# Attention with heads of 16: set-up fills, root, norm, queries and idle products put in other places

## The reference

```python
y_dca, y_main = y[:, -DCA:, :], y[:, :-DCA, :]        # DCA = 16
kv_dca = (y_dca @ Wkv_dca + bkv_dca).reshape(b, DCA, 2, H, HD)
k_dca, v_dca = _ln(kv_dca[:, :, 0], kn_dca_w, kn_dca_b), kv_dca[:, :, 1]
q = _ln((x @ Wq + bq).reshape(b, s1, H, HD), qn_w, qn_b)
kv = concat([y_main @ Wk + bk, y_main @ Wv + bv]).reshape(b, s2, H, 2 * HD)
k, v = _ln(kv[..., :HD], kn_w, kn_b), kv[..., HD:]
out = (attn(q, k, v) + attn(q, k_dca, v_dca)) @ Wo + bo   # x = x + out
```

## Time and profile before

| | |
|---|---|
| median of 3 runs | 1333.23 us (1328.89 to 1335.04) |
| the profiled execution | 1335.3 us |
| its span | 1333.6 us |
| busy share of the span: TensorE, VectorE, ScalarE, GpSimd | 88%, 76%, 65%, 25% |
| mean granted TensorE clock | 0.938 of 2.4 GHz |
| this layer's set-up, first instruction to first attention step | 326.9 to 436.5 us |

### The profile page before, as it was taken

The page is one execution under the profiler, slowest core; times in us unless marked ns, Lnnn a source line. Parts: engine busy times, 40 slices in busy tenths (PEclk is TensorE's granted clock), DMA queues, the critical chain, the costliest instruction groups (busy, mean ns, idle before and its releaser), DMA issues. The chain is left out here.

```text
span 1333.6 us, 23158 instructions
## 1 busy us (share of the span) xinstructions
PE 1167.0 (88%) x8719; PEld 772.1 (58%) x8723; DVE 1016.1 (76%) x1890; ACT 862.0 (65%) x1303; POOL 326.7 (25%) x346
## 2 busy tenths in 40 slices
PE   7999999757675787889899999888997999999997
PEld 3677677543222444557466666645883676666654
DVE  6788787396877786285789999865986898898654
ACT  5777777554344788431677677654885777777563
POOL 3000000101453000000054636500660265265200
PEclk9999999969766899879999999998999999999989
DMA  7999989102165000530699999623654999999600
GB/s 284 173 188 186 187 168 168 63 0 103 34 126 93 18 3 2 146 117 27 115 199 188 200 178 176 113 99 137 178 146 109 167 184 185 178 168 165 119 1 8
DMA packets 450834, 170.00 MB, mean 127 GB/s; under 512 B 437161, under 2 KB 437545, under 8 KB 449065
## 3 DMA queue, kind: packets, MB, share of 16 engines
q1 hardware_dynamic: 450736, 168.72, 60.9%
HBM read 58.84 MB, written 0.26 MB: 44 GB/s over the span
## 5 line engine op out<-in xcount | busy, mean ns | idle before, releaser
L462 PE MATMUL ps<-ctxT,L_xattn_qk 128*128 128x512 f16 x1152 | 268.3, 383 | 0.8 <-DVE L_xattn_mx L742 0.5
L766 DVE SCALAR_TENSOR_TENSOR arena<-L_xattn_sm,L_xattn_rr,arena 128x1024 f16<-128x1024 f32 x192 | 261.3, 1402 | 9.5 <-ACT arena L612 9.5
L597 ACT ACTIVATE L_xattn_sm<-L_xattn_sm,L_xattn_mx 128x2048 f32<-128x2048 f32 x96 | 192.2, 2003 | 73.6 <-DVE L_xattn_mx L742 71.9
L612 ACT ACTIVATE arena<-L_xattn_sm,L_xattn_rr 128x1024 f16<-128x1024 f32 x192 | 210.0, 1140 | 5.2
L462 PEld LDWEIGHTS ps<-ctxT,L_xattn_qk 128*128 128x128 f16 x1152 | 112.0, 99 | 128.7 <-issue 7.3
L484 PE MATMUL ps<-arena,ctx 128*128 128x256 f16 x1488 | 177.6, 273 | 0.0
L484 PEld LDWEIGHTS ps<-arena,ctx 128*128 128x128 f16 x1488 | 145.5, 98 | 31.8
L742 DVE CUSTOM_DVE_ANT_0 L_xattn_sm<-ps,L_xattn_bias 128x1024 f32<-128x1024 f32 x96 | 117.1, 1220 | 55.2 <-issue 55.0
L742 DVE CUSTOM_DVE_ANT_0 L_xattn_sm<-ps,L_xattn_bias,L_xattn_mx 128x1024 f32<-128x1024 f32 x96 | 123.2, 1284 | 1.7 <-DVE L_xattn_mx L742 1.1
L475 PE MATMUL ps<-arena,ctx 128*128 128x128 f16 x1488 | 100.8, 222 | 11.8 <-DMA arena<-arena 11.8
L475 PEld LDWEIGHTS ps<-arena,ctx 128*128 128x128 f16 x1488 | 92.2, 99 | 27.6 <-DMA arena<-arena 15.9
(11 more groups left out here) (584 smaller groups left out, 2163.7 us busy)
## 6 DMA issues: line engine op xcount, KB each, us to landing
L_ffn_ring<-in_L_ffn_experts SPq DMA_DIRECT2D x34, 384.0 KB, 3.6
arena<-in_L_xattn_w SPq DMA_DIRECT2D x36, 320.0 KB, 3.7
arena<-in_L_ffn_experts SPq DMA_DIRECT2D x8, 768.0 KB, 8.8
arena<-in_L_xattn_w SPq DMA_DIRECT2D x6, 640.0 KB, 7.2
arena<-arena SPq DMA_TRANSPOSE x193, 4.5
arena<-in_L_ffn_codes SPq DMA_DIRECT2D x1, 3072.0 KB, 10.9
arena<-in_L_attn_w SPq DMA_DIRECT2D x1, 2163.0 KB, 19.3
arena<-in_L_attn_w SPq DMA_DIRECT2D x2, 1026.0 KB, 5.1
```

Source lines behind the costliest of these rows:

```text
L462: last = nc.tensor.matmul(ps[:, at, :], qk[:, h // 2, qp, h % 2, b * P:(b + 1) * P], k.ctxT[:, cp, b, at * 512:(at + 1) * 512], start=(a = ...
L597: nc.scalar.activation(sm[:, u % 2, :], sm[:, u % 2, :], ACT.Exp, bias=mx[:, u % 2, 1:2], scale=-1.0, accum_out=rs[:, u % 2:u % 2 + 1]).th ...
L612: nc.scalar.mul(pp[:, u % 2, 0, at], sm[:, u % 2, at], rr[:, u % 2:u % 2 + 1]).then_inc(s.p_high, 1)
L766: nc.vector.scalar_tensor_tensor(pp[:, u % 2, 1, at], sm[:, u % 2, at], rr[:, u % 2:u % 2 + 1], pp[:, u % 2, 0, at], ALU.mult, ALU.subtrac ...
```

## The change

- GpSimd: a constant `eps` is filled at the start. Everything else waits for `b_ready`. `kstack` and `qstack` are filled with 0 only in the quarter that nothing else writes, and of `v` only the column of ones per head and the tail are filled, last.
- The root takes over the scale 1/16 and the small constant, so `variance` is the reduce alone.
- The norm of `x` moves from ahead of the groups into `beside(0)`; its root and turning follow in groups 0 and 1.
- The query products move from ahead of the loop to TensorE's group 1. All later pieces of the queries and of the small attention move one group on, on all engines and in the DMA queue. The probabilities' turning moves behind the loop.
- Idle products: 5 and 7 around the norm become 5, and three per group ahead of `products` in groups 0 to 11, in bank 5, 4 or 6.

The diff, cut to its core (in the lines left out, `gi == n` becomes `gi == n + 1` for the pieces named above):

```diff
             def _(pool):
                 done = Chain(pool, s.pool_done, 0)
                 nc.gpsimd.memset(onesh[:], 1.0).then_inc(s.set, 1)
-                done(nc.gpsimd.memset(pslot[2].bitcast(F16), 0.0))
+                nc.gpsimd.memset(eps[:], H_EPS * QUP * QUP).then_inc(s.set, 1)
+                pool.wait_ge(s.b_ready, 1)
+                done(nc.gpsimd.memset(kstack[:, :, :, :, 2, :].rearrange("p u t h d -> p (u t h) d"), 0.0))
                 for j in range(4):
                     nc.gpsimd.memset(kstack[:, :, :, j::4, 2, j:8:4].rearrange("p u t h d -> p (u t) h d"), -M_UNIT)
-                done(nc.gpsimd.memset(kstack[:, :, :, :, 2, 8:10].rearrange("p u t h d -> p (u t h) d"), 1.0))
-                nc.gpsimd.memset(v, 1.0).then_inc(s.set, 1)
+                nc.gpsimd.memset(kstack[:, :, :, :, 2, 8:10].rearrange("p u t h d -> p (u t h) d"), 1.0)
...
-                done(nc.gpsimd.memset(qstack.rearrange("p n a d -> p (n a d)"), 0.0))
+                done(nc.gpsimd.memset(qstack[:, :, 2, :], 0.0))
...
+                nc.gpsimd.memset(v_heads[:, :, :, HW:], 1.0)
+                nc.gpsimd.memset(v[:, :, NH * (HW + 1):], 0.0)
...
                 keep_busy(k, 7, 5)
-                xT_tensor(k, pe, k.xn, 4, n)
-                keep_busy(k, 7, 7)
-                pe.wait_ge(g.xnT_ready, k.xt + 1)
-                for b in range(B):
-                    for c in range(DC):
-                        last = nc.tensor.matmul(ps[:, 7, b * D:(b + 1) * D], k.xnT[:, c, b * P:(b + 1) * P],
-                                                wq[:, c, :], start=(c == 0), stop=(c == DC - 1))
-                last.then_inc(s.q_psum, 1)
                 for gi in range(GROUPS):
+                    if gi == 8:
+                        pe.wait_ge(s.d_added, 1)
+                    if gi < 12:
+                        keep_busy(k, 5 if gi < 3 else 4 if gi < 8 else 6, 3)
                     if gi + 2 < GROUPS:
                         products(gi + 2)
                         offsets(gi + 2)
+                    if gi == 0:
+                        xT_tensor(k, pe, k.xn, 4, n)
                     if gi == 1:
+                        pe.wait_ge(g.xnT_ready, k.xt + 1)
+                        for b in range(B):
+                            for c in range(DC):
+                                last = nc.tensor.matmul(ps[:, 7, b * D:(b + 1) * D], k.xnT[:, c, b * P:(b + 1) * P],
+                                                        wq[:, c, :], start=(c == 0), stop=(c == DC - 1))
+                        last.then_inc(s.q_psum, 1)
+                    if gi == 2:
                         pe.wait_ge(s.w_low, 2)
...
-                    if gi == 14:
-                        pe.wait_ge(s.dp_ready, 1)
-                        for at in range(B * DC):
-                            last = nc.tensor.transpose(ps[:, 7, at * P:(at + 1) * P],
-                                                       pd[:, 8 * at:8 * at + 8, :].rearrange("p h y -> p (h y)"), k.ident[:])
-                        last.then_inc(s.dpT_psum, 1)
+                pe.wait_ge(s.dp_ready, 1)
+                for at in range(B * DC):
+                    last = nc.tensor.transpose(ps[:, 7, at * P:(at + 1) * P],
+                                               pd[:, 8 * at:8 * at + 8, :].rearrange("p h y -> p (h y)"), k.ident[:])
+                last.then_inc(s.dpT_psum, 1)
                 pe.wait_ge(s.dpT_ready, 1)
...
             def _(act):
                 wait_weights(k, act, slot, loaded)
-                ln_scalar(k, act, n)
+                act.wait_ge(s.set, 2)
...
                     if gi >= 2:
                         act.wait_ge(turned[gi % 2], 16 * (gi // 2))
-                    else:
-                        act.wait_ge(s.pool_done, 2)
...
-                    if gi == 0:
-                        act.wait_ge(s.set, 2)
...
-                    nc.scalar.activation(kst[:, gi % 2, :], kst[:, gi % 2, :], ACT.Sqrt, bias=k.zero[:])\
+                    nc.scalar.activation(kst[:, gi % 2, :], kst[:, gi % 2, :], ACT.Sqrt, bias=eps[:],
+                                         scale=1.0 / HW)\
                         .then_inc(s.std_ready, 1)
                     if gi == 0:
-                        xT_scalar(k, act, k.xnT, 4)
+                        ln_scalar(k, act, n)
                     else:
                         keys_high(gi - 1)
+                    if gi == 1:
+                        xT_scalar(k, act, k.xnT, 4)
...
-                ln_vector(k, dve, k.x, k.xn, LN_EPS, n)
...
                 def variance(gi):
                     dve.wait_ge(s.sq_ready, gi + 1)
-                    chain(nc.vector.tensor_reduce(kst[:, gi % 2, :], sqt[:, gi % 2, :, :, :]
-                                                  .rearrange("p t h d -> p (t h) d"), AX_X, ALU.add))
-                    nc.vector.tensor_scalar(kst[:, gi % 2, :], kst[:, gi % 2, :], 1.0 / HW, H_EPS * QUP * QUP,
-                                            ALU.mult, ALU.add).then_inc(s.var_ready, 1)
+                    nc.vector.tensor_reduce(kst[:, gi % 2, :], sqt[:, gi % 2, :, :, :]
+                                            .rearrange("p t h d -> p (t h) d"), AX_X, ALU.add).then_inc(s.var_ready, 1)
...
                 def beside(gi):
 
                     if gi == 0:
+                        k.dve_n = chain.n
+                        ln_vector(k, dve, k.x, k.xn, LN_EPS, n)
+                        chain.n = k.dve_n
+                    elif gi == 1:
```

More of the change, by code:

```diff
@@ L2217, in fine_xattn_layer @@
         onesh = sb("onesh", [2, P], F16)
+        eps = sb("eps", [P, 1])
         gone = sb("gone", [P, NH], F16)
@@ L2292, in _ @@
                                             high, ALU.subtract).then_inc(s.k_low, 1)
[L2293 removed]
+                    if gi == 4:
                         pool.wait_ge(s.qn_ready, 1)
                         done(nc.gpsimd.tensor_tensor(qr, qr, row_of(qnw), ALU.mult))
[L2296 removed]
+                    if gi == 5:
                         nc.gpsimd.tensor_tensor(qr, qr, row_of(qnb), ALU.add).then_inc(s.q1_ready, 1)
                         pool.wait_ge(s.q1_ready, 1)
[L2299 removed]
+                    if gi == 6:
                         nc.gpsimd.tensor_tensor(q2.rearrange("p (b h) d -> p b (h d)", b=B), qr, row_of(knw), ALU.mult)\
@@ L2433, in _ @@
                         last.then_inc(s.d_psum, 1)
-                    if gi == 6:
+                    if gi == 7:
                         pe.wait_ge(s.q1_ready, 1)
@@ L2441, in _ @@
                         last.then_inc(s.qT_psum, 1)
-                    if gi == 9:
+                    if gi == 10:
                         pe.wait_ge(s.dn_ready, 1)
@@ L2456, in _ @@
                         last.then_inc(s.vrep_psum, 1)
-                    if gi == 11:
+                    if gi == 12:
                         pe.wait_ge(s.dm_ready, 1)
@@ L2563, in _ @@
                         nc.scalar.copy(qstack[:, :, 0, :], q2).then_inc(s.q_high, 1)
-                    if gi == 7:
+                    if gi == 8:
                         act.wait_ge(s.qT_psum, 1)
@@ L2567, in _ @@
                         nc.scalar.copy(flat(qT), ps[:, 4, :]).then_inc(s.qT_ready, 1)
-                    if gi == 8:
+                    if gi == 9:
                         act.wait_ge(s.dvar, 1)
@@ L2571, in _ @@
                             .then_inc(s.dstd, 1)
-                    if gi == 10:
+                    if gi == 11:
                         act.wait_ge(s.dT_psum, 1)
@@ L2575, in _ @@
                                              bias=cols[:, 1:2], scale=cols[:, 0:1]).then_inc(s.dT_ready, 1)
-                    if gi == 13:
+                    if gi == 14:
                         act.wait_ge(s.dcent, 1)
@@ L2659, in _ @@
                     .then_inc(s.b_ready, 1)
-                k.dve_n = chain.n
-                ln_vector(k, dve, k.x, k.xn, LN_EPS, n)
-                chain.n = k.dve_n
                 def variance(gi):
                     dve.wait_ge(s.sq_ready, gi + 1)
-                    chain(nc.vector.tensor_reduce(kst[:, gi % 2, :], sqt[:, gi % 2, :, :, :]
-                                                  .rearrange("p t h d -> p (t h) d"), AX_X, ALU.add))
-                    nc.vector.tensor_scalar(kst[:, gi % 2, :], kst[:, gi % 2, :], 1.0 / HW, H_EPS * QUP * QUP,
-                                            ALU.mult, ALU.add).then_inc(s.var_ready, 1)
+                    nc.vector.tensor_reduce(kst[:, gi % 2, :], sqt[:, gi % 2, :, :, :]
+                                            .rearrange("p t h d -> p (t h) d"), AX_X, ALU.add).then_inc(s.var_ready, 1)
                 def scale(gi):
@@ L2700, in beside @@
                         last.then_inc(s.q_added, 1)
-                    elif gi == 1:
+                    elif gi == 2:
                         dve.wait_ge(s.q_added, 1)
@@ L2713, in beside @@
                         nc.vector.tensor_tensor(qf, qf, per_head(var), ALU.mult).then_inc(s.qn_ready, 1)
```

(10 more changed lines are left out.)

21 lines of the change are left out of this document (9 added, 12 removed).

## The result

The changed kernel takes 1321.49 us (median of 8 runs, 1316.28 to 1325.39) against 1334.05 us before (8 runs): ratio 0.991, 95% interval 0.9883 to 0.9937, so 8.4 to 15.6 us less. The forecast was 1322.2. Ratios are those of executions in the chip's faster state; of all executions here one was in the slower one (2247.45 us, with the small fills first). The profiled execution of the changed kernel took 1322.07 us, with a span of 1320.3 us and a mean granted clock of 0.947.

The account below looks back on a forecast made before the run. VectorE's chain, held some 11.1 us behind GpSimd fills, was taken to bound the opening, and VectorE's order most groups. -12.8 - 0.8 + 2.4 - 2.1 + 2.25 = -11.0 us gave 1322.2 us; 8-in-10 range 1316 to 1330.

Parts of the forecast that it names:

- Part 1: Opening until `variance(0)`: fills no longer hold VectorE's `tensor_scalar`s and the norm leaves ScalarE's queue, -12.8 us.
- The cover named for the small fills: Opening: small fills at about 331.8 to 336, no `tensor_scalar` before 338, GpSimd first wanted at about 341, cost nothing.
- Part 2: Group 0, now holding the table load (1.28 us) and the norm: period 5.7 us against 6.49, -0.8.
- Part 3: Group 1: VectorE idles 3.5 us for the query products; period 7.5 us against 5.08, +2.4.
- Part 4: Groups 2 to 14, 67.99 us before: savings and moved work sum to -2.1 us.
- The root's step: Groups 2 to 14: one VectorE instruction fewer per group, -2.9 us, and 1.4 us more from executions GpSimd stretched.
- The masking's wait: Groups 2 to 14: VectorE's 3.35 us wait at line 2748 falls to 2.3 at full clock, -1.1 us.
- Part 5: Tail from `variance(15)` to the first attention step: 12.65 us against 10.39, +2.25.
- Half clock in parts: Rival, 0.17: idle products don't hold the clock; query path 2.5 us, line 2748 1.1, group 12 1.1 more; 1326.9.
- More: Rival, 0.13: TensorE keeps full clock through group 13, the tail and first steps; 1318.5 us.
- The fills only change victims: Rival, 0.05: long strided fills hold the norm and weight split, query transfer late; 7 us lost again, 1329.
- slower: Rival, 0.05: at half clock idle products stand ahead of real ones and TensorE becomes the bound; net +9, 1342 us.

Follow-up runs that it names:

- small fills first: Changed kernel with the small fills' wait for `b_ready` taken away, so they run from the start: set-up 98.80 us, whole 1324.29 us, ratio 0.9926.
- the large fills: Changed kernel with GpSimd's large fills put back from the start, first key roundings and value copy waiting again: set-up 108.88 us, whole 1332.65 us, ratio 1.001.
- the small fills alone: Kernel before with the small fills behind `b_ready`, without the waits for the large fills: set-up 99.36 us, whole 1322.21 us, ratio 0.9921.
- the last run: Changed kernel with queries' rounding later, scores ahead of products, queries' transfer earlier, exponential, division and turning in groups 13, 14, 14: set-up 87.54 us, whole 1313.36 us.
- small attention earlier: Changed kernel with the small attention's pieces, from the turning of its keys on, one group earlier: set-up 99.67 us, whole 1319.98 us, ratio 0.9897.

## Why the prediction was right, point by point

- **Part 1, the opening.** -12.93 against -12.8, and shown three ways: the holds vanish, come back with the large fills (+11.6), and the small fills alone give 10.2. The cover named for the small fills held: they run from 333.83 to 338.03, GpSimd's first group work starts at 342.77, and no `tensor_scalar` of VectorE's falls between. Their length was 4.2 us (estimate 4), though the strided ones cost more than the 0.88 ns per element that I took. One reading was off: line 2656 does not end as a fill ends but at 342.14, 0.28 us behind one (339.78 to 341.86), with the rest of its own 0.47 us still to do. The holds sum to 11.0 us all the same.
- **Part 2.** -0.86 against -0.8. The root follows the value copy (which ends at 335.99) and the load of 1.28 us at once, at 337.31; in group 15 the load starts 0.02 us behind the activation in front of it too (413.55 and 413.57) and takes 1.28 us. A switch cost 1.3 us here, and nothing like a drain of 1.4 us stands beside it, with ScalarE just at work. The 2.66 us of the Trainium skill, page ScalarE: Activation LUTs, section What ACT_TABLE_LOAD costs, would have been 2.8 us too much over the two loads, by an estimate.
- **Part 3, the queries' wait.** +1.82 against +2.4. The wait was 2.13 us, not 3.5. The term was mis-sized at both of its ends:

```profile
343.44 1.47 PE L2329 MATMUL ps<-arena,ctxT 128*128 128x512 f16 x6 [0.82 <-DVE L_xattn_p L2679]
...
343.74 1.53 DVE L2700 SCALAR_TENSOR_TENSOR arena<-arena 128x512 f16<-128x512 f32 x1
...
345.37 1.99 PE L2433 MATMUL ps<-arena,xnT 128*128 128x256 f32 x8
...
347.40 0.76 DVE L2704 TENSOR_TENSOR L_xattn_ks<-ps,arena 128x256 f32<-128x256 f32 x2 [2.13 <-PE ps L2433]
```

  Group 3's products and offsets took 2.0 us where I had 2.6 (two gaps that did not come), which is the 0.6 us of the period. VectorE's second split instruction took 1.53 us beside GpSimd's work instead of the 0.69 of the kernel before, so VectorE itself came later and waited less. The four transposes took 0.66 us at full clock, not the 1.11 of a row at half clock, but nothing came of it: TensorE waited 0.82 us for VectorE behind them.
- **Part 4.** -2.36 against -2.1, close by cancelling. The root's step ("-2.9" and "1.4 us more") was too large as a gain of the set-up: putting the instruction back costs 1.3 us, since more than half of what it saves ends in the waits of groups 11 to 13. The masking's wait went to 1.09 us, not 2.3. That it was TensorE's clock was right, but I counted the small products alone. From the start of the products ahead of the turning to its end TensorE took 5.94 us before and 3.16 after, 2.78 less, and VectorE's body between is 0.52 us shorter, which leaves the measured 2.26. What held the clock there was not the idle products: without them it is 1.00 in groups 10 and 11 too, the masking waits the same 1.09 us, and the set-up is 0.4 us shorter. And the statement that no idle stretch ahead of group 12 passes 2.3 us was wrong by my own numbers for group 7; it was 2.94 us, the clock fell to 0.71, and nothing waited for that. The key rounding's wait for a transfer (1.39 us in front of group 11's square) I had not seen; it moves GpSimd's remainder beside the second masking product, which costs 0.6 us. Group 12's long wait came as said, 5.21 us for 4.9, but the queries' transfer had about 0.2 us of cover, not two.
- **Part 5, the tail.** +2.01 against +2.25; the chain behind the loop is as listed. That the tail was the price of moving the softmax is shown by the last run, 10.2 us with it back; 0.8 us of that come back as a longer group 14.
- **Rivals.** *Half clock in parts* did not come: ahead of group 12 the clock fell in groups 8 and 9 alone (0.71 and 0.83), and of the three things it prices the queries' path and the masking ran at 1.00. In group 12 it was 0.67, and the wait 0.3 us longer than forecast, not 1.1. Where runs did have a low clock, most groups kept their length because VectorE's order hides it, and groups 4 and 10 did not. *More* did not come, group 13 and the tail ran at 0.50. *The fills only change victims* did not come, as part 1 shows. The *slower* rival's mechanism exists, in three of the runs: with the clock at or near 0.50 the three idle products stand in front of real ones in groups 4 and 10 (both runs with fills first) and in groups 9 and 10 (small attention earlier).

The sum was right to 1.3 us, with its one large term right to 0.1 and its smaller ones partly by luck. That the whole program's median came within 0.7 us of the forecast is luck too: the gain was 12.6 us instead of 11.0, and the median before rose from 1333.23 to 1334.05 with more runs. That the idle products don't pay was decided by the runs, not by the prediction; what the small attention's move is worth at full clock stays open.

## What to carry to other kernels

Read a busy engine's rows for instructions that take far longer than their size: a `tensor_scalar` of 16 elements with 6.65 us was a GpSimd fill of 9,216 elements, and small fills in another place, alone, took 10.2 of the 12.3 us. Put fills behind the chain that starts a stage, and fill only what nothing else writes. Before adding idle products, or moving work to save a wait, ask which queue the wait ends in: here 9 us more lay in the order of three queues (scores behind products that nobody was waiting for, ScalarE's rounding in front of its next square, the queries' transfer behind one more of the keys'). And before putting a difference down to an edit, compare the clock of the two runs ahead of it.

## What the runs showed of the hardware that I had not expected

- A held `tensor_scalar` can be passed over twice: beside small fills, one of 0.17 us took 1.32 us, through a fill of 0.95 us that had started 0.10 us ahead of it and the next one of 0.56 us. It ended 0.04 us behind the second.
- Two-input operations kept their time beside fills (0.69 us) but not always beside GpSimd's work on the keys: one of 0.69 us took 1.53 us, four of 0.89 us together took 1.47.
- Fills of 512 single elements 17 apart took 0.94 us, of the same number in runs of 16 0.56 us, of 1,024 in runs of 16 half-precision elements 0.95 us; per element 1.8, 1.1 and 0.9 ns.
- The course of TensorE's clock through 97 us of set-up repeated in a second profile (all groups within 0.03). Yet it is not given by the order of work alone: with the small fills first, TensorE idled the same 2.33 us ahead of group 4's products as in the changed kernel, behind the same list, and those six took 1.85 us against 1.47 and the next two 1.03 against 0.60; with the small attention earlier the clock in group 9 was 0.50 instead of 0.83. What decides between the two no run here separates.
